# Turning quantised token and FFN rows with transposing DMAs in place of TensorE transposes

## The chip, the cores and the metric

The kernel runs on one core of a Trainium2 chip. The metric is the time of one execution on the device in microseconds (us); of a kernel that was run several times it is the median.

## The reference

`x` and `ctx` are [16, 256, 512] in float32. One cross-attention layer with 8 heads is followed by one FFN whose activations and weights are quantised. The heads split the rows of a batch element: head h takes rows 32h to 32h+31 of the queries, the keys and the values, and the attention is over the 512 columns.

```
def xattn(q, k, v):                     # q = layernorm(x), k = v = ctx
    qh, kh, vh = (a.reshape(16 * 8, 32, 512) for a in (q, k, v))
    sm = softmax(einsum('bdm,bdn->bmn', qh, kh) / sqrt(32), axis=-1)
    return einsum('bmn,bcn->bcm', sm, vh).reshape(16, 256, 512)

def act_quant(x):                       # per row: round(x * 127 / max|x|), scaled back
    scale = 127.0 / clip(max(abs(x), axis=-1, keepdims=True), 1e-5)
    return clip(round(x * scale), -128, 127) / scale

def bitlinear(x, w):                    # weights become -1, 0 or 1 times one scale
    return einsum('bsd,fd->bsf', act_quant(x), weight_quant(w))

x = x + xattn(layernorm(x), ctx, ctx)
x = x + bitlinear(silu(bitlinear(layernorm(x), W1)), W2)      # W1 [2048, 512], W2 [512, 2048]
```

## The kernel before, in words

The 4096 token rows are cut into 32 tiles of 128 rows (4 heads of 32 rows). A tile passes through these stages, and several tiles are in flight at once:

- Preparation: the tile of x and of ctx is loaded (`load`), x is normalised (`stats_x`, `aggregate`, `moments`, `rstd`, `xn`), ctx is scaled (`key_squares`, `key_norm`, `key_scale`, `key_rsqrt`), and both are split into two f16 parts (`qh`, `ql`, `kh`, `kl`), which small DMAs stack on partitions (`stack_qh` and the others).
- Maxima: 16 matmuls of 512 columns (`maxima`, tile mxp), each read by VectorE (`max_read`). The maxima of the rows are turned by one TensorE transpose (`ct`) and written back as two rows (`crow`) that the scores subtract.
- Scores: 16 matmuls into `st`, 16 exponentials on ScalarE, 8 pair sums on GpSimd (`sums`), the products with the values (`values`, tile pv) and the denominators (`denominators`, tile dn), then division (`invert`, `attend`), the residual sum on GpSimd (`residual`), and the second norm (`norm2`, `rstd2`, `xn2`).
- FFN: the row maximum (`absmax2`), a factor (`scale2`, `scale2_b`), `quantise` on GpSimd, the turn of the [128, 512] rows (`xqt`), a conversion to f16 on ScalarE (`xqt_evac`), four groups of four matmuls against W1 (`first`), `tanh` on ScalarE and `gate` on VectorE for each of the four parts, the maximum over all four (`hidden_max`, `hidden_scale` to `hidden_scale_d`), the quantisation of 2048 values a row, two parts of 512 on GpSimd (`hidden_quantise`) and two on ScalarE (`quantise_act`), the turn of [128, 2048] in two halves (`ht`, `ht_evac`), four groups of four matmuls against W2 (`second`), `rescale`, `finish`, `store`.

Each engine has its own instruction stream, written out by one loop: a tile has 16 units, one score matmul (TensorE) or exponential (ScalarE) in each, and the table `PLAN` says in which unit, counted from the first score of the tile, an engine carries out a step. A step at 28 lies in the second tile period after its own tile's first score. Within a unit the lists in `ORDER` decide. An engine takes its steps strictly in this order, and semaphores hold each until its inputs are there, so an engine's unit is a place in its queue and not a time. All DMAs are issued by the queue of the sync engine (SP), also in the order of the plan.

Before the change, quantising is the addition of a large constant (`MAGIC`), after which the low 16 bits of each float32 are an f16 number offset by 1536. TensorE turns these 128x128 blocks with an identity matrix into the PSUM bank `bank_a`: 4 blocks for the tokens, 8 for each half of the FFN rows. ScalarE then reads the bank, takes the offset off and writes f16 into `xqt` or `hqt`. The bank is shared with `key_norm`, `ct` and two of the four `first` groups, and the function `bank_free` puts a wait ahead of each use.

Of the kernel before, what the change touches and what calls it, by code (L numbers as in the profile page):

```python
# [6 lines left out]
B, S, D = 16, 256, 512  # L7
HEADS = 8
DH = S // HEADS
F = 2048  # L10
# [29 lines left out]
    key_squares=[-48],  # L40
    key_norm=[-41],
    stats_x=[-40],
    aggregate=[-39],
    rstd=[-41],
    xn=[-39],
    key_scale=[-41],
    kh=[-38],
    qh=[-31],
    kl=[-37],
    ql=[-35],  # L50
    maxima=[-22, -22, -21, -20, -20, -18, -17, -16, -15, -12, -11, -10, -10, -9, -8, -8],
    ct=[-6],
    ct_evac=[-6],
    ct_low=[-6],
    values=[13, 17, 19, 19],
    sums=[-2, 2, 4, 4, 6, 6, 6, 6],
    denominators=[17, 17],
    invert=[19],
    attend=[20],
    residual=[11],  # L60
    norm2=[21],
    norm2b=[23],
    rstd2=[17],
    xn2=[17],
    absmax2=[25],
    scale2=[25],
    quantise=[20],
    xqt=[27],
    xqt_evac=[26],
    first=[28, 28, 31, 32],  # L70
    tanh=[28, 28, 31, 32],
    gate=[29, 30, 32, 33],
    hidden_max=[30, 31, 34, 35],
    hidden_scale=[35],
    hidden_quantise=[26, 26],
    ht=[37, 39],
    ht_evac=[37, 39],
    second=[39, 40, 41, 42],
    finish=[39],
    max_read=[-22, -21, -21, -20, -20, -18, -18, -17, -13, -11, -11, -11, -10, -8, -7, -7],  # L80
    key_scale_b=[-3],
    moments=[-37],
    moments2=[24],
    scale2_b=[26],
# [3 lines left out]
    hidden_scale_c=[36],  # L88
    hidden_scale_d=[36],
    rescale=[42],  # L90
    quantise_act=[35, 37],
    key_rsqrt=[-46],
    load=[-56],
    load_v=[11],
    stack_qh=[-30],
    stack_kh=[-30],
    stack_ql=[-28],
    stack_kl=[-31],
    xr=[10],
    crow=[-2],  # L100
    store=[46],
# [5 lines left out]
    load=[-46, -43, -40, -35, -23, -20, -19, -19],  # L107
    rows=[-36, -35, -12, -9],
    abs=[-32, -25, -24, -24, -14, -9, -9, -7],
    sum=[-29, -7],  # L110
    quantise=[-24, -23, -22, -21, -7, -6, -5, 4],
    convert=[-23, -21, -16, -15, -4, -3, -1, 6],
# [4 lines left out]
ORDER = {'pool': ['xn', 'residual', 'rstd', 'hidden_quantise', 'key_rsqrt', 'rstd2', 'ql', 'quantise', 'sums',  # L117
          'xn2', 'finish'],
 'act': ['ht_evac', 'tanh', 'quantise_act', 'ct_evac', 'qh', 'kh', 'rescale', 'xqt_evac', 'key_squares'],
 'dve': ['hidden_scale_c', 'invert_b', 'scale2_b', 'gate', 'hidden_scale_d', 'key_scale_b', 'hidden_max',  # L120
          'max_read', 'kl', 'norm2', 'moments2', 'invert_c', 'key_scale', 'hidden_scale', 'absmax2',
          'moments', 'hidden_scale_b', 'norm2b', 'invert', 'stats_x', 'ct_low', 'attend', 'scale2',
          'aggregate'],
 'pe': ['key_norm', 'maxima', 'values', 'ct', 'xqt', 'first', 'denominators', 'second', 'ht'],
 'sp': ['xr', 'stack_kh', 'crow', 'stack_ql', 'store', 'stack_qh', 'load', 'stack_kl', 'load_v']}
# [41 lines left out]
def build(nc, x, ctx_in, values_t, w1t_in, w2t_in, out):  # L167
    f32 = mybir.dt.float32
    f16 = mybir.dt.float16
    ALU = mybir.AluOpType  # L170
# [10 lines left out]
    with stack:  # L181
# [32 lines left out]
        xqt = sb("xqt", [P, NC, P], f16)  # L214
# [79 lines left out]
        xqm_done = sem("xqm_done")  # L294
# [22 lines left out]
        xqt_done = sem("xqt_done")  # L317
# [6 lines left out]
        ht_done = sem("ht_done")  # L324
# [18 lines left out]
        def _(sp):  # L343
# [63 lines left out]
            def run(slot):  # L407
                steps = {"load": load, "load_v": load_values, "stack_qh": stack_qh, "stack_kh": stack_kh, "stack_ql": stack_ql,
                         "stack_kl": stack_kl, "xr": residual_rows, "crow": maxima_rows, "store": store}
# [14 lines left out]
            for b in range(-3, TILES + 3):  # L424
                run(Slot(b))
# [13 lines left out]
        BANK_A = uses(("key_norm", 0, key_clamped, 1, 1), ("ht", 0, ht_evac, 2, 1), ("ht", 1, ht_evac, 2, 2),  # L439
                      ("ct", 0, ct_low, 1, 1), ("xqt", 0, xqt_evac, 1, 1),  # L440
# [16 lines left out]
        def _(pool):  # L457
# [68 lines left out]
            def quantise(slot, off):  # L526
                r = slot.ring(off)
                wait(pool, token_scale, slot, 1, off, 1)
                pool.tensor_scalar(xqm[:, r % 2, :], xn2[:, :], sm2[:, r, SQ:SQ + 1], MAGIC, ALU.mult, ALU.add).then_inc(xqm_done, 1)

            def hidden_quantise(slot, off, n):

                if n == 0:
                    wait(pool, hidden_factor, slot, 1, off, 1)
                part = hu[:, 2 * n * D:(2 * n + 1) * D]
                pool.tensor_scalar(part, part, sm3[:, slot.ring(off), QS:QS + 1], MAGIC,  # L536
                                   ALU.mult, ALU.add).then_inc(hq_done, 1)
# [17 lines left out]
            for b in range(-3, TILES + 2):  # L555
                run(Slot(b))

        @block.scalar
        def _(act):
# [32 lines left out]
            def hidden_evac(slot, off, g):  # L592


                wait(act, ht_done, slot, 2, off, g + 1)
# [68 lines left out]
            for b in range(-3, TILES + 2):  # L664
                run(Slot(b))
# [332 lines left out]
```

## Time and profile before

| | |
|---|---|
| median of 3 runs | 803.3 us (802.32 to 803.55) |
| the profiled execution, its own time | 802.65 us |
| its span in the trace | 800.9 us |
| TensorE matmuls, busy | 724.1 us, 90% |
| VectorE, busy | 721.5 us, 90% |
| ScalarE, busy | 634.3 us, 79% |
| GpSimd, busy | 606.1 us, 76% |
| DMA queue of SP | 75.79 MB, 33.3% of the 16 engines |

PE is the matmul side of TensorE, PEld its weight load, DVE VectorE, ACT ScalarE, POOL GpSimd, SPq the queue of the sync engine. Busy shares are over the whole span, in which the first 60 us hold the weights' preparation and the last 36 us the drain of the pipeline. A matmul's record lasts longer than the distance to the next one, since matmuls are pipelined.

### The profile page before, as it was taken

How to read it: one execution, taken by the hardware profiler on the slowest of the kernel's cores; microseconds unless marked ns; L12 is line 12 of the kernel's file. 1: busy time of each engine (PE TensorE's matmuls, PEld its weight loads, DVE VectorE, ACT ScalarE, POOL GpSimd, SP SyncE). 2: the span in 40 equal slices, each digit the busy share in tenths (PEclk: the TensorE clock that was granted, in tenths of full speed). 3: DMA queues.
4: the chain of work that ended last, by engine and by line, in shares of the span. 5: the costliest groups of instructions: out<-in, count | busy, mean ns of one | idle time of the engine just before them, and what ended most of it. 6: DMA issues, size and time to landing. Idle time of an engine off the chain costs nothing.

```text
span 800.9 us, 13866 instructions
## 1 busy us (share of the span) xinstructions
PE 724.1 (90%) x4324; PEld 276.8 (35%) x4324; DVE 721.5 (90%) x1596; ACT 634.3 (79%) x1017; POOL 606.1 (76%) x619
## 2 busy tenths in 40 slices
PE   0349999999999999999999999999999999999984
PEld 0012233333333333333333333333333333333332
DVE  1898899999999999999999999999999999998552
ACT  4567688888888888888888888888888888877853
POOL 2215778888898888888889888888888988887861
PEclk9999899999999999999999999999999999999998
DMA  8553223233233333323323333333332333331100
GB/s 294 191 133 98 91 75 101 75 85 103 88 83 106 106 107 106 100 74 87 103 88 82 107 107 106 106 92 80 88 103 88 83 106 106 81 80 41 41 19 21
DMA packets 53960, 76.66 MB, mean 96 GB/s; under 512 B 7808, under 2 KB 32384, under 8 KB 52864
## 3 DMA queue, kind: packets, MB, share of 16 engines
q1 hardware_dynamic: 53888, 75.79, 33.3%
q8 instruction: 35, 0.57, 0.3%
q14 instruction: 37, 0.30, 0.1%
HBM read 41.94 MB, written 8.39 MB: 63 GB/s over the span
## 4 chain that ended last, share of the span: by engine, by line
PE 75%; DVE 8%; ACT 8%; issue 3%; DMA 3%; POOL 1%; SPq 1%; POOLq 0%; ACTq 0%; DVEq 0%
PE pv L893 15%; PE bank_b L924 13%; PE st L873 12%; PE mxp L883 11%; PE bank_b L953 7%; PE bank_a L953 7%; PE dn L902 7%; DVE mx L708 4%; ACT probs L569 4%; ACT late L596 3%; DMA late<-w 2%; PE bank_a L912 2%; PE bank_a L930 1%; DVE late L827 1%; DVE late L829 1%
## 5 line engine op out<-in xcount | busy, mean ns | idle before, releaser
L569 ACT ACTIVATE probs<-st,sm 128x512 f32<-128x512 f32 x512 | 333.7, 685 | 51.3 <-PE st L873 51.1
L502 POOL TENSOR_TENSOR sums<-probs 128x512 f32<-128x512 f32 x256 | 322.3, 1275 | 44.6 <-ACT probs L569 44.5
L708 DVE TENSOR_REDUCE mx<-mxp 128x1 f32<-128x512 f32 x512 | 335.1, 679 | 11.4 <-PE mxp L883 9.2
L883 PE MATMUL mxp<-ks,qs 96*128 96x512 f16 x512 | 195.5, 402 | 32.7 <-DVE mx L708 25.7
L873 PE MATMUL st<-qs,ks 98*128 98x512 f16 x512 | 195.0, 393 | 1.4 <-ACT probs L569 1.4
L924 PE MATMUL bank_b<-w2t,late 128*128 128x512 f16 x512 | 132.6, 382 | 3.0 <-ACT late L596 3.0
L893 PE MATMUL pv<-probs,vt 128*32 128x512 f32 x1024 | 130.6, 605 | 0.0
L883 PEld LDWEIGHTS mxp<-ks,qs 96*128 96x128 f16 x512 | 52.9, 104 | 117.3 <-DVE mx L708 87.1
L536 POOL TENSOR_SCALAR late<-late,sm 128x512 f32<-128x512 f32 x64 | 43.7, 696 | 60.4 <-DVE sm L808 60.4
L873 PEld LDWEIGHTS st<-qs,ks 98*128 98x128 f16 x512 | 47.8, 99 | 115.4 <-issue 55.3
L782 DVE TENSOR_REDUCE hmx<-late 128x1 f32<-128x512 f32 x128 | 83.4, 673 | 0.0
L596 ACT ACTIVATE late<-bank_a 128x1024 f16<-128x1024 f16 x64 | 65.6, 1025 | 13.7 <-PE bank_a L912 13.7
L924 PEld LDWEIGHTS bank_b<-w2t,late 128*128 128x128 f16 x512 | 49.4, 97 | 57.0 <-ACT late L596 4.9
L953 PE MATMUL bank_b<-w1t,xqt 128*128 128x512 f16 x256 | 66.3, 381 | 2.5 <-ACT xqt L612 1.8
L953 PE MATMUL bank_a<-w1t,xqt 128*128 128x512 f16 x256 | 65.7, 379 | 0.0
L902 PE MATMUL dn<-sums,ones 128*32 128x512 f32 x512 | 60.8, 592 | 0.0
L777 DVE SCALAR_TENSOR_TENSOR late<-late,bank_b 128x512 f32<-128x512 f32 x64 | 43.1, 674 | 14.9 <-ACT late L621 14.9
L590 ACT CAST qh<-xn 128x512 f16<-128x512 f32 x32 | 19.8, 618 | 41.7 <-POOL xn L485 41.7
L621 ACT ACTIVATE late<-bank_b,sm 128x512 f32<-128x512 f32 x64 | 44.0, 687 | 10.0 <-PE bank_b L953 8.3
L621 ACT ACTIVATE late<-bank_a,sm 128x512 f32<-128x512 f32 x64 | 44.0, 688 | 10.0 <-PE bank_a L953 7.2
L602 ACT ACTIVATE late<-late,sm 128x512 f32<-128x512 f32 x64 | 46.3, 723 | 6.2 <-DVE sm L808 6.2
L512 POOL TENSOR_TENSOR late<-att,xr 128x512 f32<-128x512 f32 x32 | 40.6, 1268 | 10.5 <-DVE att L733 10.5
(77 smaller groups left out, 913.4 us busy)
## 6 DMA issues: line engine op xcount, KB each, us to landing
cs<-ctx SPq DMA_DIRECT2D x32, 256.0 KB, 3.0
xs<-x SPq DMA_DIRECT2D x32, 256.0 KB, 3.6
late<-w SPq DMA_DIRECT2D x8, 1024.0 KB, 6.9
ks<-kh SPq DMA_DIRECT2D x64, 128.0 KB, 3.3
qs<-qh SPq DMA_DIRECT2D x64, 128.0 KB, 3.6
xr<-x SPq DMA_DIRECT2D x32, 256.0 KB, 4.1
vt<-values_t SPq DMA_DIRECT2D x32, 256.0 KB, 3.9
out<-late SPq DMA_DIRECT2D x32, 256.0 KB, 2.0
```

Source lines behind the costliest of these rows:

```text
L502: pool.tensor_tensor(sums[:, pair, h, :], probs[:, 2 * pair, h, :], probs[:, 2 * pair + 1, h, :], ALU.add).then_inc(sum_done, 1)
L569: act.activation(probs[:, c, h, :], st[u % 2][:, :], ACT.Exp, scale=sm1[:, r, ESC:ESC + 1]).then_inc(exp_done, 1)
L596: act.activation(hqt[:, FG // 2 * g:FG // 2 * (g + 1), :], bank_a[:, :].bitcast(f16).rearrange("p (c t) -> p c t", t=P), ACT.Copy, bias=-O ...
L621: act.activation(th[:, fc % 2, :], bank[:, :], ACT.Tanh, scale=sm2[:, slot.ring(off), HZ:HZ + 1]).then_inc(tanh_done, 1)
L708: dve.reduce_max(mx[:, slot.ring(off), NC * h + c:NC * h + c + 1], mxp[m % 2][:, :], axis=AX.X).then_inc(max_done, 1)
L782: dve.tensor_reduce(out=hmx[:, slot.ring(off), fc:fc + 1], in_=hu[:, fc * D:(fc + 1) * D], axis=AX.X, op=ALU.max, apply_absolute_value=Tru ...
L873: pe.matmul(st[u % 2][:, :], ks[0:3 * DH + 2, r, h, c * P:(c + 1) * P], qs[0:3 * DH + 2, r, h, :], start=True, stop=True).then_inc(st_done, 1)
L883: pe.matmul(mxp[m % 2][:, :], qs[0:3 * DH, r, h, c * P:(c + 1) * P], ks[0:3 * DH, r, h, :], start=True, stop=True).then_inc(mx_done, 1)
L893: last = pe.matmul(pv[DH * h:DH * (h + 1), :], vt[:, k, c, DH * h:DH * (h + 1)], probs[:, c, h, :], start=(c == 0), stop=(c == NC - 1), sk ...
L902: last = pe.matmul(dn[DH * h:DH * (h + 1), :], ones[:, 0:DH], sums[:, pair, h, :], start=(pair == 0), stop=(pair == 1), skip_group_check=True)
L924: last = pe.matmul(bank_b[:, :], hqt[:, f, :], w2t[:, f, :], start=(f == 0), stop=(f == FG - 1))
L953: last = pe.matmul(bank[:, :], xqt[:, j, :], w1t[:, j, fc * D:(fc + 1) * D], start=(j == 0), stop=(j == NC - 1))
```

## The change

The quantised rows are written as 16-bit integers (the conversion rounds), and DMAs on SP turn them from SBUF to SBUF. ScalarE reads the turned integers from SBUF and writes f16, for the tokens in place and for the FFN rows in place too. The 20 TensorE transposes of a tile and their use of `bank_a` are gone. One token DMA turns [128, 512], two hidden DMAs turn [128, 1024] each. New waits guard the buffers, and `PLAN`, `WEIGHTS` and `ORDER` are laid out anew.

```diff
+        xq = sb("xq", [P, 2, D], i16)
+        xqi = sb("xqi", [P, NC, P], i16)
+        xqt = xqi[:, :, :].rearrange("p c t -> p (c t)").bitcast(f16).rearrange("p (c t) -> p c t", t=P)
-        xqm = late[:, 8 * D:10 * D].rearrange("p (r d) -> p r d", d=D)
+        hq = late[:, 8 * D:10 * D].bitcast(i16)
+        hqi = late[:, 14 * D:16 * D].bitcast(i16).rearrange("p (g t) -> p g t", t=P)
...
+            def tokens_transpose(slot, off):
+                wait(sp, xq_done, slot, 1, off, 1)
+                wait(sp, f1_done, slot, FC, off - 1, FC)
+                sp.dma_start_transpose(out=xqi[:, :, :], in_=xq[:, slot.ring(off) % 2, :]).then_inc(xqt_landed, 16)
+            def hidden_transpose(slot, off, g):
+                wait(sp, hq_done, slot, 2, off, g + 1)
+                wait(sp, hqa_done, slot, 2, off, g + 1)
+                wait(sp, f2_done, slot, FC, off - 1, FC)
+                sp.dma_start_transpose(out=hqi[:, FG // 2 * g:FG // 2 * (g + 1), :],
+                                       in_=hq[:, F // 2 * g:F // 2 * (g + 1)]).then_inc(ht_landed[g], 16)
...
-                pool.tensor_scalar(xqm[:, r % 2, :], xn2[:, :], sm2[:, r, SQ:SQ + 1], MAGIC, ALU.mult, ALU.add).then_inc(xqm_done, 1)
+                wait(pool, xqt_landed, slot, 16, off - 2, 16)
+                pool.tensor_scalar(xq[:, r % 2, :], xn2[:, :], sm2[:, r, SQ:SQ + 1], 1.0, ALU.mult, ALU.mult).then_inc(xq_done, 1)
...
+                wait(pool, ht_landed[n], slot, 16, off - 1, 16)
+                pool.tensor_scalar(hq[:, part], hu[:, part], sm3[:, slot.ring(off), QS:QS + 1], 1.0,
+                                   ALU.mult, ALU.mult).then_inc(hq_done, 1)
...
-                act.activation(hqt[:, FG // 2 * g:FG // 2 * (g + 1), :], bank_a[:, :].bitcast(f16).rearrange("p (c t) -> p c t", t=P),
-                               ACT.Copy, bias=-OFFSET).then_inc(ht_evac, 1)
+                wait(act, ht_landed[g], slot, 16, off, 16)
+                act.copy(hqt[:, part, :], hqi[:, part, :]).then_inc(ht_evac, 1)
...
+                wait(act, ht_landed[n], slot, 16, off - 1, 16)
+                act.activation(hq[:, part], hu[:, part], ACT.Copy, scale=sm3[:, slot.ring(off), QS:QS + 1]).then_inc(hqa_done, 1)
...
+                wait(act, xqt_landed, slot, 16, off, 16)
+                act.copy(xqt, xqi[:, :, :]).then_inc(xqt_evac, 1)
...
-                    wait(dve, ht_done, slot, 2, off - 1, 2)
+                    wait(dve, hq_done, slot, 2, off - 1, 2)
+                    wait(dve, hqa_done, slot, 2, off - 1, 2)
```

The places in the plan of the steps that the prediction speaks of (before, then after):

```diff
-    values=[13, 17, 19, 19],          attend=[20],  residual=[11], quantise=[20],
+    values=[11, 17, 17, 17],          attend=[21],  residual=[18], quantise=[21],
-    xqt=[27],      xqt_evac=[26],     first=[28, 28, 31, 32],      gate=[29, 30, 32, 33],
+    xqt=[26],      xqt_evac=[26],     first=[28, 29, 31, 31],      gate=[30, 32, 33, 33],
-    hidden_quantise=[26, 26],         quantise_act=[35, 37],       hidden_scale_d=[36],
+    hidden_quantise=[31, 32],         quantise_act=[33, 34],       hidden_scale_d=[36],
-    ht=[37, 39],   ht_evac=[37, 39],  second=[39, 40, 41, 42],     store=[46],
+    ht=[35, 38],   ht_evac=[39, 40],  second=[40, 40, 41, 42],     store=[55],
-    load=[-56],    load_v=[11],       xr=[10],      crow=[-2],
+    load=[-54],    load_v=[9],        xr=[9],       crow=[-5],
```

In the order of SP's queue, the units of a period now hold: 0 `stack_qh`, `stack_ql`; 3 `ht` of the first half; 6 `ht` of the second; 7 `store`; 9 `xr`, `load_v`; 10 `load`, `xqt`; 11 `crow`; 12 `stack_kh`; 14 `stack_kl`.

## Rows read from the trace of the kernel before

**Rows 1.** The profile's page: busy time of the engines.

```profile
PE 724.1 (90%) x4324; PEld 276.8 (35%) x4324; DVE 721.5 (90%) x1596; ACT 634.3 (79%) x1017; POOL 606.1 (76%) x619
```

**Rows 2.** Busy time of each engine in stretches of time.

```profile
core 0: us, PE busy (x) PEld busy (x) DVE busy (x) ACT busy (x) POOL busy (x), PEclk, DMA share, GB/s
400.11:422.35 22.24, 21.82 (x137) 8.52 (x135) 21.75 (x50) 18.76 (x32) 18.69 (x20) 1.00 0.34 95
...
700.00:764.40 64.40, 61.74 (x388) 23.07 (x388) 48.52 (x112) 52.41 (x83) 50.31 (x50) 1.00 0.18 50
764.40:800.90 36.50, 22.75 (x134) 9.25 (x133) 14.69 (x37) 14.01 (x19) 13.51 (x14) 0.91 0.06 22
```

**Rows 3.** The chain that ended last, 400.11 to 422.35 us (start, length).

```profile
402.74 0.45 PE bank_a L912 x8
```

**Rows 4.** Waits of VectorE, 120 to 700 us (total, times, longest).

```profile
DVE mx L708 <- PE mxp L883: 5.8, 26, 0.2
```

**Rows 5.** Groups of instructions by line, whole span.

```profile
L912 PE MATMUL bank_a<-idh,late 128*128 128x128 f16 x512 | 39.9, 222 | 4.8 <-POOL late L536 4.8
L941 PE MATMUL bank_a<-idh,late 128*128 128x128 f16 x128 | 12.6, 221 | 0.6 <-POOL late L529 0.4 <-DVE crow L713 0.2
L596 ACT ACTIVATE late<-bank_a 128x1024 f16<-128x1024 f16 x64 | 65.6, 1025 | 13.7 <-PE bank_a L912 13.7
L612 ACT ACTIVATE xqt<-bank_a 128x512 f16<-128x512 f16 x32 | 19.1, 597 | 1.3 <-PE bank_a L941 1.2
L590 ACT CAST qh<-xn 128x512 f16<-128x512 f32 x32 | 19.8, 618 | 41.7 <-POOL xn L485 41.7
L529 POOL TENSOR_SCALAR late<-xn,sm 128x512 f32<-128x512 f32 x32 | 22.2, 695 | 1.2 <-DVE sm L767 1.2
L494 POOL TENSOR_TENSOR ql<-xn,qh 128x512 f16<-128x512 f32 x32 | 37.5, 1171 | 9.3 <-ACT qh L590 9.3
```

**Rows 6.** Timeline of one period: from the attention's division to the second FFN product.

```profile
398.58 0.69 DVE L733 TENSOR_TENSOR att<-pv,rden 128x512 f32<-128x512 f32 x1
...
406.38 0.69 POOL L529 TENSOR_SCALAR late<-xn,sm 128x512 f32<-128x512 f32 x1
...
408.86 1.03 PE L953 MATMUL bank_b<-w1t,xqt 128*128 128x512 f16 x4
...
401.71 1.03 PE L924 MATMUL bank_b<-w2t,late 128*128 128x512 f16 x4
...
419.81 0.13 DVE L808 TENSOR_SCALAR sm<-sm 128x1 f32<-128x1 f32 x1
```

**Rows 7.** DMA issues by line, KB each, median us from issue to landing.

```profile
xs<-x SPq DMA_DIRECT2D x32, 256.0 KB, 3.6
ks<-kl SPq DMA_DIRECT2D x32, 128.0 KB, 3.0
qs<-crow SPq DMA_DIRECT2D x64, 4.0 KB, 1.7
```

**Rows 8.** Landing times of the xr loads, the longest of the bulk in steady work.

```profile
DMA to landing us min/median/max: 2.7/4.1/4.6
```

**Rows 9.** Timeline of the last tile's drain.

```profile
777.31 0.69 POOL L529 TENSOR_SCALAR late<-xn,sm 128x512 f32<-128x512 f32 x1 [1.20 <-DVE sm L767]
...
779.15 1.04 PE L953 MATMUL bank_b<-w1t,xqt 128*128 128x512 f16 x4 [0.69 <-ACT xqt L612]
...
787.28 1.37 POOL L536 TENSOR_SCALAR late<-late,sm 128x512 f32<-128x512 f32 x2 [7.59 <-DVE sm L808]
...
790.18 1.89 PE L924 MATMUL bank_b<-w2t,late 128*128 128x512 f16 x4 [1.12 <-ACT late L596]
...
791.86 1.06 PE L912 MATMUL bank_a<-idh,late 128*128 128x128 f16 x8
...
792.72 3.55 PE L924 MATMUL bank_b<-w2t,late 128*128 128x512 f16 x12
```

More of the change, by code:

```diff
@@ L87 @@
     hidden_scale_b=[35],
-    hidden_scale_c=[36],
+    hidden_scale_c=[35],
     hidden_scale_d=[36],
     rescale=[42],
[L91 to L101, printed above, removed]
+    quantise_act=[33, 34],
+    key_rsqrt=[-42],
+    load=[-54],
+    load_v=[9],
+    stack_qh=[-32],
+    stack_kh=[-36],
+    stack_ql=[-32],
+    stack_kl=[-34],
@@ L102 @@
+    xr=[9],
+    crow=[-5],
+    store=[55],
 )
 WEIGHTS = dict(
[L107 to L112, printed above, removed]
-)
[L117 to L125, printed above, removed]
+    load=[-47, -43, -38, -37, -19, -18, -15, -9],
@@ new lines @@
+    rows=[-48, -31, -10, -9],
+    abs=[-39, -31, -31, -29, -15, -11, -10, -7],
+    sum=[-26, -4],
+    quantise=[-24, -21, -18, -13, -3, -2, 0, 3],
+    convert=[-21, -21, -14, -13, -7, -6, 2, 11],
+)
+ORDER = {'pool': ['rstd', 'hidden_quantise', 'ql', 'sums', 'residual', 'rstd2', 'finish', 'xn', 'key_rsqrt', 'xn2',
+          'quantise'],
+ 'act': ['qh', 'ct_evac', 'rescale', 'quantise_act', 'key_squares', 'ht_evac', 'xqt_evac', 'kh', 'tanh'],
+ 'dve': ['hidden_max', 'scale2_b', 'aggregate', 'max_read', 'stats_x', 'kl', 'invert_b', 'gate', 'ct_low',
+          'norm2', 'key_scale', 'absmax2', 'moments', 'scale2', 'hidden_scale', 'hidden_scale_d', 'invert',
+          'attend', 'norm2b', 'hidden_scale_b', 'moments2', 'key_scale_b', 'hidden_scale_c', 'invert_c'],
+ 'pe': ['first', 'maxima', 'denominators', 'key_norm', 'second', 'ct', 'values'],
+ 'sp': ['load', 'stack_qh', 'stack_ql', 'xqt', 'xr', 'ht', 'stack_kh', 'store', 'load_v', 'crow',
+          'stack_kl']}
@@ L423, in _ @@
                 fetch(Slot(t), 0)
-            for b in range(-3, TILES + 3):
+            for b in range(-3, TILES + 4):
                 run(Slot(b))
@@ L904, in denominators @@
                 last.then_inc(dn_done, 1)
-            def hidden_transpose(slot, off, g):
-                wait(pe, hq_done, slot, 2, off, g + 1)
-                wait(pe, hqa_done, slot, 2, off, g + 1)
-                bank_free(pe, BANK_A, slot, off, place("ht", g))
-                for j in range(FG // 2):
-                    f = FG // 2 * g + j
-                    last = pe.transpose(bank_a[:, :].bitcast(f16)[:, j * P:(j + 1) * P],
-                                        low_half(hu[:, f * P:(f + 1) * P]), idh[:, :])
-                last.then_inc(ht_done, 1)
             def second(slot, off, g):
@@ L935, in maxima_transpose @@
                 pe.transpose(bank_a[:, 0:P], mx[:, slot.ring(off), :], idf[:, :]).then_inc(ct_done, 1)
-            def tokens_transpose(slot, off):
-                wait(pe, xqm_done, slot, 1, off, 1)
-                bank_free(pe, BANK_A, slot, off, place("xqt", 0))
-                for j in range(NC):
-                    last = pe.transpose(bank_a[:, 0:D // 2].bitcast(f16)[:, j * P:(j + 1) * P],
-                                        low_half(xqm[:, slot.ring(off) % 2, j * P:(j + 1) * P]), idh[:, :])
-                last.then_inc(xqt_done, 1)
             def first(slot, off, fc):
```

121 lines of the change are left out of this document (57 added, 64 removed).

## The prediction

> **What bounds the kernel now.** I read the page first: TensorE and VectorE are both busy for 90% of the span, ScalarE and GpSimd clearly less [rows 1]. That is an average over ramp, steady work and drain, so the windows come next. One steady tile period is 22.24 us. In it PE is busy for 21.82 us and VectorE for 21.75 us [rows 2]: two engines stand almost wall to wall, with 0.42 and 0.49 us left, while ScalarE has 3.5 us and GpSimd 3.55 us of air. The clock is at full speed there (1.00, the 2.4 GHz level), so no gain is to be had from it in steady work.
>
> The chain of waits tells which of the two sets the pace. It runs on TensorE for most of the period, and the eight transposes of half the FFN rows occupy 0.45 us of it, 0.056 us each [rows 3]. That is much less than the 0.222 us that a record of one lasts [rows 5], since matmuls are pipelined: the 640 records sum to 52.5 us, but on the chain they are worth 640 x 0.056 = 36 us at the most. VectorE's own waits show the other side: over 26 periods it waited for TensorE only 26 times, for 5.8 us, all at the maxima [rows 4]. The rest of its 0.49 us are short gaps between its own dependent instructions.
>
> **The change part by part.**
>
> *Removed from TensorE.* Two halves of 0.45 us and the tokens' four blocks, 4 x 0.056 = 0.22 us: 1.12 us a period. TensorE could then run a period in 22.24 - 1.12 = 21.12 us. VectorE gets no instruction less: a gate waits for the quantisers instead of the transposes, that is all. So VectorE is next, at 21.75 us plus its own gaps. What can be had in steady work is its wait for TensorE, 5.8 / 26 = 0.22 us a period, over 26 periods -5.8 us. Bounds: 0 (the wait turns into another one of the same length), and all of the 0.49 us, 26 x 0.49 = -12.7 us. I take -5.8, the wait that names TensorE.
>
> *Last scores, 700 to 764 us.* No maxima are left, VectorE is busy for 48.5 of 64.4 us, PE for 61.7 [rows 2]. Two to three tiles' transposes lie on the path; at 1.12 us each, two tiles are -2.2 us. ScalarE and GpSimd at 52 and 50 us are not far off and their order is changed, so I take half, -1.1, between 0 and -2.2.
>
> *Conversions.* ScalarE reads SBUF in place of PSUM. A cast of 512 columns from SBUF takes 618 ns against 597 from PSUM [rows 5]: 0.02 us more for the tokens, at twice the width 0.04 for each half, 0.1 us a period, which its 3.5 us of air take; without them it would be 26 x 0.1 = 2.6 us. GpSimd writes 16-bit integers instead of f32; no row shows this form. The f16 output of the nearest operation with conversion is not slower (1171 ns for ql, with two inputs), so I keep 695 ns; the upper bound is 1171, +0.48 us for each of three, 1.4 us a period out of 3.55 us of air.
>
> *Added to SP's queue.* Three issues a period. The existing ones go out in 0.35 to 0.65 us, about twelve of them are 7 us of 22, so three more fit, if an issue is like the others. `xqt` and `ht` wait for their quantisers. Behind `ht` stand `store`, `xr`, `load_v` and `load`, which are read a tile or more later; behind `xqt` stands `crow`, five units ahead of the scores that need it (about 7 us against 1.7 us of landing [rows 7]). I cost these at nothing; the cover is that lead.
>
> *Added to the latency.* This is the part that decides. Before, the tokens' quantised rows are ready at 407.07, and the first product starts at 408.86 [rows 6]. From the division (399.27) to that product are 9.6 us, of which 7.8 go by to the end of the quantiser. In the new plan the last values' products stand two units earlier (17 for 19) with `first` still at 28; a unit is 22.24 / 16 = 1.39 us, so some 2.5 us are won and 12.1 us are there. Less 7.8, and less 0.6 for the conversion, the DMA may take about 3.7 us. For the FFN rows: the factor is ready at 419.94 and the second product starts at 401.71 + 22.24 = 423.95 [rows 6], 4.0 us later; with the last `first` one unit earlier and `second` one later there are 6.7 us, less 0.7 for quantising and 1.1 for conversion: about 4.9 us for the landing.
>
> No row shows a transposing DMA. Bounds from the plain ones: 1.7 us (the 4 KB rows) to 4.6 us (the longest bulk load) [rows 7, 8]. The tokens' 128 KB are nearest to the stack of kl, 128 KB in SBUF, 3.0 us; the halves' 256 KB to the load of xs, 3.6 us [rows 7]. I take 3.0 and 3.5. Both fit their places, with 0.7 and 1.4 us to spare. ScalarE, which takes the conversion in order ahead of later exponentials, may wait for it; its air covers that up to the same limit.
>
> One rule of the Trainium skill speaks against this. "VectorE: DVE Perf Modes", section "The three transpose paths", gives 390 ns to a 128x128 block on TensorE and 1309 ns to one by DMA, and advises TensorE where PSUM will do. Our row of a TensorE transpose, 222 ns, is shorter still; if the blocks of a DMA came one after the other at that figure, the tokens' four would be an estimated 5.2 us and a half's eight 10.5 us. "Advanced Engine Details and Errata", section "X-Bar Transpose (TRN2)", says the opposite of the rate: as fast as regular DMAs, which would leave my 3.0 and 3.5 us. No row here decides between them.
>
> *The drain.* The last tile is one chain, in which the longer latency is not hidden. Tokens: from the quantiser's end at 778.00 to the product at 779.15 are 1.15 us [rows 9]; with 3.0 + 0.6 + 0.1 it is 3.7, +2.6 us. FFN rows: the first part is ready at 787.97, the product starts at 790.18, 2.2 us; with 3.5 + 1.0 + 0.2 it is 4.7, +2.5 us. The transposes amid the second product go, 791.86 to 792.72: -0.85 us. Together +4.3 us. With 1.7 and 4.6 us for both DMAs it would be +1.2 and +7.0.
>
> *Sum.* -5.8 - 1.1 + 4.3 = -2.6 us, on the profiled execution's 802.65 us (span 800.9 and 1.75 around it): 800.05. That execution lay 0.65 below the median of 803.3, so 800.7 is what I forecast for the median. Its own range: -12.7 - 2.2 + 1.2 gives 789.6, and 0 + 0 + 7.0 gives 810.3; the middle of it, 795 to 806, holds most.
>
> **The rivals.**
>
> *A: the tokens' DMA lands after its place (slower).* Place: ScalarE's `xqt_evac`, then `first`. What speaks for it: SP issues `xr`, `load_v` and two loads of 256 KB just ahead of `xqt`; bulk loads in such a row land up to 4.6 us after issue [rows 8], above the 3.7 us. And a 16-bit turn moves small pieces. Against: the loads may have drained when the quantiser is ready. It decides from 3.7 us on: each microsecond above it holds `first`, `tanh`, `gate` and with it VectorE back once a period, 29 periods or so. At 4.6 us: 0.9 x 29 = +26 us in place of -5.8, with the drain's +6 about 829 us; at 5.2 us about 848. It begins gently, at about 806.
>
> *B: the turn is slow in itself or occupies SP for long (slower by much).* If the halves need 8 us, 3.1 above their 4.9, each period grows by that: 29 x 3.1 = +90 us, some 900 us. The share of the DMA engines, 0.34 [rows 2], gives no ground for it, but no row excludes it. This is where the first rule of the skill above would lead.
>
> *C: the full gain.* VectorE closes all its gaps thanks to the new order, and the drain costs little: 790 to 794 us. Against: most of its gaps follow from its own dependences, which are unchanged.
>
> *D: integer output is slow on GpSimd.* With +1.4 us a period GpSimd is at 20.1 of 22 us, which alone fits, but 0.48 us come off each of the two places above; it then acts as rival A does and shares its chance.
>
> **How the numbers follow.** A difference of 0.2%, 1.6 us, is about what a measurement of this kernel can tell from none. My forecast holds 0.48 (of it 0.28 below 801.7 us, 0.12 between 801.7 and 804.9, 0.08 above). A with D has 0.37, all slower, mostly between 806 and 848. B has 0.10, C 0.05. Faster 0.33, same 0.12, slower 0.55: the single likeliest case is a small gain, but more of the chance lies on the side of a loss, since the gain is capped by VectorE and the loss by nothing. The range reaches from 793 to 845: it leaves out C's half, B, and the end of A.
>
> **What would show it.** Right: a period between 21.8 and 22.1 us, VectorE at 99% of it, PE at 95% or less, no wait for PE at the maxima, landings of about 3 and 3.5 us, the drain after the last score some 4 us longer. Wrong: ScalarE waiting for `xqt` or the FFN rows' DMA in each period, VectorE waiting for tanh at the first gate (A); landings above 5 us or transposing issues of several us on SP (B); records of the quantisers on GpSimd well above 0.7 us (D). The step most likely to fail is the landing time, which I had to take from DMAs that turn nothing.

## The result, and the profile after

The changed kernel takes 862.7 us (median of 4, 859.9 to 866.1) against 803.4 us before: 1.073 times as long (95% interval 1.071 to 1.076). The forecast was 800.7 us with a range of 793 to 845. The landing times of the new DMAs came out close to what was forecast; the period did not.

The page of the changed kernel answers to [rows 1]; its second part shows the clock.

```profile
PE 757.2 (88%) x3684; PEld 244.8 (28%) x3684; DVE 709.9 (82%) x1596; ACT 640.4 (74%) x1017; POOL 608.7 (71%) x619
...
PEclk9999799999999999999999999999999999999887
```

PE carries out 640 matmuls less and is busy 33 us longer. VectorE fell from 90% to 82% of the span: it isn't the bound that the prediction took it for. In a steady period it is busy for 21.1 to 21.3 us, against 21.75 before [rows 2], with the same instructions; the section on one_block says why. Two periods of the changed kernel, the third tile's and a later one, by the view of stretches (columns as in [rows 2]):

```profile
136.15:158.85 22.70, 21.52 (x117) 7.26 (x115) 21.10 (x50) 18.90 (x32) 18.80 (x19) 1.00 0.50 127
231.25:255.15 23.90, 22.84 (x116) 7.61 (x115) 21.20 (x50) 18.91 (x32) 18.81 (x19) 0.93 0.47 117
```

They hold the same instructions. The second is 1.2 us longer, and what differs is the granted clock, 1.00 against 0.93. The starts of the residual sums, one a tile, lie 22.8, 22.7, 22.7 us apart at the beginning, then 24.2, 24.2, 24.0, 24.0 and 23.9 to the end of steady work (22.24 before). Seven of the sixteenths of one such period show where the clock goes:

```profile
398.76:400.25 1.49, 0.98 (x5) 0.23 (x4) 1.49 (x3) 1.49 (x4) 1.26 (x1) 1.00 1.28 154
400.25:401.75 1.50, 1.46 (x5) 0.28 (x5) 1.43 (x6) 1.50 (x3) 0.14 (x1) 1.00 0.78 151
401.75:403.24 1.49, 1.12 (x4) 0.23 (x3) 1.42 (x3) 1.49 (x3) 1.38 (x3) 0.67 0.98 259
403.24:404.74 1.50, 1.50 (x5) 0.50 (x4) 1.47 (x7) 1.12 (x3) 1.20 (x2) 0.50 0.95 354
404.74:406.23 1.49, 1.49 (x6) 0.57 (x5) 1.49 (x3) 0.81 (x1) 1.49 (x2) 0.69 0.79 205
406.23:407.72 1.49, 1.49 (x9) 0.66 (x8) 0.65 (x2) 0.67 (x1) 1.49 (x3) 1.00 0.76 190
407.72:409.22 1.50, 1.50 (x9) 0.77 (x8) 0.78 (x2) 1.05 (x4) 1.50 (x2) 1.00 0.05 10
```

The granted clock is 1.00 (2.4 GHz), falls to 0.50 (1.2 GHz) and returns within 4 us. Ahead of the fall, PE has only four or five matmuls in 1.5 us. In the low stretch stand the first eight matmuls of the second FFN product; the timeline (start, length) has them as

```profile
404.03 2.70 PE L934 MATMUL bank_b<-w2t,late 128*128 128x512 f16 x8
```

and the chain of waits as

```profile
404.24 2.50 PE bank_b L934 x8
```

2.50 us for eight, where four take 0.86 us at full clock. That is 0.8 of the 1.2 us; the scores and maxima in the low stretch take longer as well. Right behind, VectorE, which had been the busy one, runs dry: in the timeline

```profile
405.69 0.68 DVE L691 BATCH_NORM_STATS2 bn<-xs 128x6 f32<-128x512 f32 x1
407.21 0.69 DVE L727 TENSOR_REDUCE mx<-mxp 128x1 f32<-128x512 f32 x1 [0.84 <-PE mxp L903]
408.62 0.69 DVE L727 TENSOR_REDUCE mx<-mxp 128x1 f32<-128x512 f32 x1 [0.72 <-PE mxp L903]
```

From 240 to 700 us it waited for the maxima's matmuls 46.7 us in all, 2.4 us a period, against 5.8 us in 26 periods in [rows 4]. Not all of that is the clock: in fill_8 (below), whose clock stays at 1.00, 28.5 us of it remain, 1.4 us a period. First the changed kernel, then fill_8:

```profile
DVE mx L727 <- PE mxp L903: 46.7, 80, 1.0
...
DVE mx L728 <- PE mxp L904: 28.5, 60, 0.7
```

The new operations, by groups of instructions:

```profile
L556 POOL TENSOR_SCALAR late<-late,sm 128x512 int16<-128x512 f32 x64 | 43.6, 695 | 12.5 <-DVE sm L828 12.1
L615 ACT CAST late<-late 128x1024 f16<-128x1024 int16 x64 | 66.2, 1035 | 6.2 <-DMA late<-late 6.2
L549 POOL TENSOR_SCALAR xq<-xn,sm 128x512 int16<-128x512 f32 x32 | 22.2, 693 | 9.1 <-DVE sm L786 8.3
```

and the new DMAs, in the page's part on DMA issues (median us from issue to landing at the end):

```profile
late<-late SPq DMA_TRANSPOSE x64, 3.2
xqi<-xq SPq DMA_TRANSPOSE x32, 2.9
```

ScalarE waited for a transposing DMA four times in the whole execution, 6.2 us together. Integer output costs GpSimd nothing (695 and 693 ns against 695 in [rows 5]).

**Where the 60.8 us of the span are.** By the residual sums: start of the first one +3.1 us; three first periods +1.2; 26 steady periods +44.1, that is some 12 from the nearly 0.5 us by which even a period at full clock is longer, and 32 from the clock; the last two periods +5.6; from the last residual sum to the end +6.8 (35.5 against 28.8).

### The profile page after: what moved, and what is told of

The parts are those of the page before. It is cut to its first block, busy times and chain, and to the rows that moved or that the text cites. A ratio compares the mean times of both kernels' runs of the same rounds, so it can differ in the third digit from the quotient of the medians.

```text
span 861.7 us, 12835 instructions
## 1 busy us (share of the span) xinstructions
PE 757.2 (88%) x3684; PEld 244.8 (28%) x3684; DVE 709.9 (82%) x1596; ACT 640.4 (74%) x1017; POOL 608.7 (71%) x619
## 2 busy tenths in 40 slices
DMA packets 138950, 97.58 MB, mean 113 GB/s; under 512 B 92800, under 2 KB 117376, under 8 KB 137856
## 4 chain that ended last, share of the span: by engine, by line
DVE 50%; PE 39%; issue 6%; DMA 2%; POOL 2%; ACT 1%; SPq 0%; POOLq 0%; ACTq 0%
DVE mx L727 17%; PE bank_b L934 15%; PE mxp L903 9%; DVE late L797 8%; DVE hmx L802 8%; PE st L893 6%; PE pv L913 5%; PE bank_b L955 3%; DVE att L752 2%; DVE bn L757 2%; DVE dspread L738 2%; DVE rden L746 2%; DMA late<-w 2%; DVE late L849 1%; DVE late L847 1%
## 5 line engine op out<-in xcount | busy, mean ns | idle before, releaser
L520 POOL TENSOR_TENSOR sums<-probs 128x512 f32<-128x512 f32 x256 | 322.4, 1272 | 29.7 <-ACT probs L589 28.9
L903 PE MATMUL mxp<-ks,qs 96*128 96x512 f16 x512 | 206.4, 431 | 40.1 <-DVE mx L727 39.3
L934 PE MATMUL bank_b<-w2t,late 128*128 128x512 f16 x512 | 156.0, 448 | 14.2 <-ACT late L615 14.2
L934 PEld LDWEIGHTS bank_b<-w2t,late 128*128 128x128 f16 x512 | 57.5, 113 | 99.0 <-issue 44.6
L622 ACT ACTIVATE late<-late,sm 128x512 int16<-128x512 f32 x64 | 45.6, 716 | 44.2 <-DVE sm L828 44.2
L615 ACT CAST late<-late 128x1024 f16<-128x1024 int16 x64 | 66.2, 1035 | 6.2 <-DMA late<-late 6.2
L490 POOL TENSOR_TENSOR sm<-sm,half 128x1 f32<-128x1 f32 x32 | 19.5, 609 | 70.2 <-DVE sm L704 70.2
L955 PE MATMUL bank_b<-w1t,xqi 128*128 128x512 f16 x256 | 65.8, 378 | 2.0 <-ACT xqi L632 1.3
L955 PE MATMUL bank_a<-w1t,xqi 128*128 128x512 f16 x256 | 66.0, 380 | 0.0
L535 POOL TENSOR_TENSOR sm<-sm,half 128x1 f32<-128x1 f32 x32 | 17.6, 549 | 50.1 <-DVE sm L770 50.1
L562 POOL TENSOR_TENSOR late<-late 128x512 f32<-128x512 f32 x32 | 41.3, 1292 | 15.9 <-ACT late L649 15.9
L556 POOL TENSOR_SCALAR late<-late,sm 128x512 int16<-128x512 f32 x64 | 43.6, 695 | 12.5 <-DVE sm L828 12.1
```

Source lines behind the costliest of these rows:

```text
L520: pool.tensor_tensor(sums[:, pair, h, :], probs[:, 2 * pair, h, :], probs[:, 2 * pair + 1, h, :], ALU.add).then_inc(sum_done, 1)
L615: act.copy(hqt[:, part, :], hqi[:, part, :]).then_inc(ht_evac, 1)
L903: pe.matmul(mxp[m % 2][:, :], qs[0:3 * DH, r, h, c * P:(c + 1) * P], ks[0:3 * DH, r, h, :], start=True, stop=True).then_inc(mx_done, 1)
L934: last = pe.matmul(bank_b[:, :], hqt[:, f, :], w2t[:, f, :], start=(f == 0), stop=(f == FG - 1))
L955: last = pe.matmul(bank[:, :], xqt[:, j, :], w1t[:, j, fc * D:(fc + 1) * D], start=(j == 0), stop=(j == NC - 1))
```

## The experiments

Each kernel ran against the kernel before on the same chip. "Period" is the distance of the residual sums' starts in steady work (where it varies, its range and the mean of the 26 periods from the fourth on), "clock" the mean granted one there.

| run | us | ratio to before (95%) | period, us | clock |
|---|---|---|---|---|
| changed kernel | 862.7 | 1.073 (1.071 to 1.076) | 23.9 | 0.93 |
| small_copy | 855.8 | 1.064 (1.061 to 1.067) | 23.9 | 0.93 |
| plain_copy | 857.0 | 1.066 (1.063 to 1.069) | 22.7 and 23.9 | 1.00 and 0.93 |
| fill_8 | 828.5 | 1.031 (1.029 to 1.034) | 22.7 | 1.00 |
| fill_old | 838.6 | 1.044 (1.042 to 1.046) | 23.2 | 1.00 |
| fill_gap | 840.6 | 1.046 (1.042 to 1.049) | 23.1 | 1.00 |
| fill_late | 868.1 | 1.080 (1.076 to 1.083) | 23.8 | 1.00 |
| one_block | 790.5 | 0.983 (0.981 to 0.985) | 21.74 | 1.00 |
| tokens_only | 865.2 | 1.074 (1.070 to 1.078) | 22.9 to 25.2, mean 24.2 | 0.98 |
| hidden_only | 1012.8 | 1.260 (1.258 to 1.262) | 28.8 to 30.2 | 0.86 to 0.89 |
| pe_after_plan | 1008.3 | 1.255 (1.253 to 1.257) | 28.3 and 29.7 in turn | 0.91 |
| values_spread | 972.6 | 1.210 (1.208 to 1.213) | 27.4, some up to 28.9 | 0.89 to 0.92 |
| replan_fill | 877.3 | 1.091 (1.088 to 1.094) | 23.9 to 25.9, mean 24.3 | 0.99 |
| replan_nofill | 890.1 | 1.106 (1.103 to 1.109) | 23.5 to 26.9, mean 25.1 | 0.94 |
| replan2_fill | 933.1 | 1.158 (1.152 to 1.164) | 24.5 to 28.4, mean 26.1 | 0.94 |
| replan3_fill | 825.5 | 1.026 (1.024 to 1.028) | 22.1 to 23.7, mean 22.5 | 1.00 |
| replan3_nofill | 839.5 | 1.043 (1.039 to 1.047) | 22.1 to 24.2, mean 22.9 | 0.98 |
| replan4_fill | 835.7 | 1.037 (1.033 to 1.041) | 22.8 to 24.4, mean 23.1 | 1.00 |

### Are the DMAs themselves the cost? plain_copy and small_copy

```diff
-                sp.dma_start_transpose(out=xqi[:, :, :], in_=xq[:, slot.ring(off) % 2, :]).then_inc(xqt_landed, 16)
+                part = slice(0, D if slot.b + off == 0 else 8)          # small_copy; plain_copy: all of D
+                sp.dma_start(xqi[:, :, :].rearrange("p c t -> p (c t)")[:, part], xq[:, slot.ring(off) % 2, part]).then_inc(xqt_landed, 16)
```

and the same for the two DMAs of the FFN rows. Both leave the turn out, so the FFN works on other values; queues and waits stay.

> The changed kernel with plain DMAs of the same bytes in place of the transposing ones (the rows aren't turned, so the FFN's values are wrong; sizes, queues and waits stay). If transposing as such costs time (issue of 1.25 us in place of 0.6, small packets, DMA share 0.48): faster by 5 us or more. If plan, clock and place in the period are the cause: within 3 us of the changed kernel, 860 to 866.

> The changed kernel with plain DMAs of 16 bytes a partition in place of the transposing ones (from the second tile on; the FFN's values are wrong), which should land in about 2 us in place of 2.9 and 3.2 and load the DMA engines hardly at all. If the landing time sets the period: 2 x 1 us a period come back, 800 to 830. Plan and clock theory: the period stays at 23.5 to 23.9 us, and only the drain gets some 2 to 3 us shorter: 850 to 860.

The DMA issues of small_copy:

```profile
late<-late SPq DMA_DIRECT2D x62, 2.0 KB, 1.8
...
xqi<-xq SPq DMA_DIRECT2D x31, 2.0 KB, 1.7
```

and two of its periods, by the view of stretches:

```profile
400.00:423.90 23.90, 22.99 (x116) 7.52 (x115) 21.32 (x50) 18.98 (x32) 18.81 (x19) 0.93 0.30 89
423.90:447.80 23.90, 22.98 (x116) 7.52 (x115) 21.33 (x50) 18.97 (x32) 18.82 (x19) 0.93 0.32 90
```

The landings are 1.2 and 1.4 us shorter, the DMA share falls from 0.48 to some 0.31, and the period is 23.90 us as in the changed kernel, to the hundredth. With this plan, landing time, packets, load and the time of issue of the transposing DMAs have no part in the steady loss; they are worth the 7 us by which the whole gets shorter, nearly all of it after the last residual sum (30.0 us against 35.5). That sinks the prediction's rivals A and B, and the first of the rules it weighed: "VectorE: DVE Perf Modes" of the Trainium skill, section "The three transpose paths", would have made four blocks 5.2 us; the measured DMA of four blocks lands after 2.9 us, issue included.

plain_copy is 5.7 us faster than the changed kernel, which by its expectation spoke for a cost of the turn itself. By the residual sums it comes from the start (2.4 us), from three more periods that stay short (3.5) and from the end (3.3), not from a shorter steady period. It shows something else. Its periods switch between two lengths in one execution, with the same instructions (the view of stretches again):

```profile
204.70:227.40 22.70, 21.51 (x117) 7.28 (x115) 21.09 (x51) 18.93 (x32) 18.80 (x19) 1.00 0.43 123
...
296.90:320.90 24.00, 22.92 (x117) 7.61 (x115) 21.25 (x51) 19.00 (x32) 18.79 (x19) 0.93 0.38 116
```

### Is it the clock? fill_gap, fill_old, fill_8, fill_late

Transposes of the identity are added, into the half of the bank `dn` that nothing reads then. Only their number and place differ: 7 in each of the units 3 to 7 (fill_gap); 8, 8 and 4 in units 5, 7 and 11, where the removed ones had been (fill_old); 4 and 4 in units 4 and 6 (fill_8); 10 and 10 in units 9 and 11 (fill_late).

```diff
+            def fill(slot, off, n):
+                wait(pe, dn_spread, slot, 1, off - 1, 1)
+                for j in range((4, 4)[n]):
+                    pe.transpose(dn[:, D // 2:].bitcast(f16)[:, (j % NC) * P:(j % NC + 1) * P], idh[:, :], idh[:, :])
```

> The changed kernel with 35 extra 128-column TensorE transposes of the identity a period (7 in each of the units 3 to 7, into the unused half of bank dn; the output is unaffected). Clock theory (the thin stretch of TensorE in units 2 to 7 makes the granted clock fall, and the second FFN product that follows runs at half speed, 1.65 us a period): the clock stays at 1.00 in steady work, the period falls from 23.9 to about 22.3 us, the time to 810 to 825. Order theory (too much TensorE work is crowded into units 8 to 15 and VectorE starves there at any clock): period 23.5 us or more, 855 or more. DMA theory (transposing DMAs delay their readers or the stacks): unchanged, 860 to 866, or slower by the work added.

> The changed kernel with 20 extra transposes of the identity a period, as many as the change took away and at their old places (8 in unit 5, 8 in unit 7, 4 in unit 11), into the unused half of bank dn. If the removed transposes by themselves kept the clock up: as fill_gap, 810 to 825. If the thinness comes from the moved values' products rather than from the transposes: the clock still falls, 855 to 865. DMA theory: 860 to 870.

> The changed kernel with 8 transposes of the identity a period, 4 in unit 4 and 4 in unit 6. If 0.45 us of work in the thin stretch hold the clock: period 22.7 to 22.9 us (the changed kernel's own period where its clock was 1.00, tiles 2 and 3, is 22.7), 825 to 832 in all. If it takes more to hold it: still 0.93 and 23.9 us, 860 to 866.

> The changed kernel with 20 transposes of the identity a period, as many as in fill_old, but 10 in unit 9 and 10 in unit 11, where TensorE is dense. Place theory: the thin stretch stays thin, the clock falls as in the changed kernel, and the added 1.1 us lie on the path: 24.5 to 25.5 us a period, 880 to 915. Count theory (matmuls in a period hold the clock wherever they are): clock 1.00, 23.2 to 23.9 us, 838 to 862.

A period of fill_8:

```profile
400.00:422.70 22.70, 21.79 (x127) 7.75 (x126) 21.09 (x51) 18.89 (x32) 18.78 (x20) 1.00 0.53 122
```

With 0.45 us of useless work a period (eight transposes at the 0.056 us of [rows 3]), the clock stays at 1.00 and the kernel is 34 us faster than the changed one. Its period, 22.7 us, is that of the changed kernel's own first periods. So the clock's fall costs 1.2 us a period, about 31 us over the 26 steady ones, and this is shown by adding work alone. fill_gap and fill_old fell short of their expected 810 to 825 us: the clock held, but the period stayed above 23 us, of which 0.4 to 0.5 are due to the added work. One of my own expectations fell too: I had put the fall down to the thin stretch alone. In fill_late that stretch is as thin as ever and the clock still stayed at 1.00; only its 1.1 us of work lie on the path (22.7 + 1.1 = 23.8), which puts its time between the ranges of both theories:

```profile
400.00:424.00 24.00, 22.82 (x139) 8.37 (x135) 21.28 (x51) 19.27 (x33) 18.97 (x21) 1.00 0.47 118
```

What keeps the clock up is therefore not settled by these runs. Shown are that it falls in the thin stretch, that it does so in some periods and not in others with the same instructions (plain_copy: three to five matmuls in 1.5 us ahead of the second FFN product in both), and that in this plan added TensorE work in either place prevented it. It is no general cure: in replan2_fill, another plan, the clock fell to 0.50 in spite of 20 added transposes a period (0.94 in the mean).

### What is removing the transposes worth? one_block

The kernel before, with 3 of the 20 transposes of a tile left, so the FFN works on other values.

```diff
-                for j in range(FG // 2):
+                for j in range(1):
...
-                for j in range(NC):
+                for j in range(1):
```

> The kernel before with only one of the 8 or 4 transposes of each turn carried out; the conversions read that one block for all, so the FFN's inputs are wrong in value while every wait, read and write stays. It is what removing the transposes alone is worth, with no DMA and the plan unchanged (17 of 20 gone). By the prediction's step: TensorE has 0.95 us less a period and VectorE sets the pace, 22.0 us a period, 795 to 798 in all. If thinning TensorE by itself brings the clock down: a dip in each period, 805 or more. If VectorE's waits don't shrink: 803.

A period of one_block, by the view of stretches:

```profile
394.91:416.65 21.74, 20.94 (x120) 7.60 (x118) 20.99 (x50) 18.59 (x32) 19.13 (x19) 1.00 0.35 97
```

and its group of instructions for `kl`:

```profile
L702 DVE SCALAR_TENSOR_TENSOR kl<-cs,sm,kh 128x512 f16<-128x512 f32 x32 | 23.9, 748 | 0.7 <-ACT kh L583 0.7
```

It comes out faster than expected: 790.5 us, 0.983 of before. The period falls by 0.50 us, where I had 0.22. VectorE's waits for the maxima account for that 0.22; its busy time falls as well, from 21.75 to 20.99 us, although it has the same instructions. Nearly all of this is one instruction: `kl` took 1464 ns on average before and takes 748 ns here. So the 0.50 us is not the freed TensorE time alone: without the transposes `kl` also starts at another place beside GpSimd's work.

What that place does can be read in the timelines (start, length). In the kernel before, `kl` starts 1.0 us ahead of the end of a pair sum on GpSimd; in replan3_fill it starts 0.9 us ahead in one period and 0.2 us ahead in another:

```profile
407.04 2.49 POOL L502 TENSOR_TENSOR sums<-probs 128x512 f32<-128x512 f32 x2
408.50 1.58 DVE L702 SCALAR_TENSOR_TENSOR kl<-cs,sm,kh 128x512 f16<-128x512 f32 x1
...
376.42 1.27 POOL L550 TENSOR_TENSOR sums<-probs 128x512 f32<-128x512 f32 x1
376.75 1.49 DVE L751 SCALAR_TENSOR_TENSOR kl<-cs,sm,kh 128x512 f16<-128x512 f32 x1
...
217.87 1.29 POOL L550 TENSOR_TENSOR sums<-probs 128x512 f32<-128x512 f32 x1
218.93 0.79 DVE L751 SCALAR_TENSOR_TENSOR kl<-cs,sm,kh 128x512 f16<-128x512 f32 x1
```

Each time `kl` ends 0.55 us behind the sum. In nine traces there are 223 `kl` that start with 0.2 us or more of a two-input GpSimd operation on 128x512 left to run, and all of them end 0.54 to 0.56 us behind it, whatever their own length; with nothing beside it, one takes 0.74 us. It also goes the other way: in one_block at 403.65 us `kl` takes 0.74 us, and the sum that starts 0.13 us after it is recorded with 1.74 us in place of 1.27. No run moves `kl` alone, but the lengths leave little else. The changed plan is clear of this too (`kl` 765 ns, VectorE 0.65 us a period less than before), so VectorE had more room than the prediction gave it, and the period still grew.

The clock is 1.00: with the plan of before, taking the work away doesn't bring it down.

### Is it the plan? values_spread, pe_after_plan, hidden_only, tokens_only

```diff
-    values=[11, 17, 17, 17],
+    values=[11, 17, 19, 19],      # values_spread: the changed kernel, nothing else
```

pe_after_plan is the kernel before with the changed plan (`xqt` at 27, `ht` at 39 and 40 on TensorE). hidden_only and tokens_only keep the plan of before and turn one of the two by DMA.

> The changed kernel with two of the four groups of values' products moved from unit 17 to unit 19 (values = 11, 17, 19, 19; before the change 13, 17, 19, 19), which puts 16 real matmuls into the thin stretch. Clock theory: the stretch is fuller, the dip shorter or gone, 815 to 845, though the division comes some 2 us later and the tokens' DMA lands nearer to its reader. Order theory: some gain too, from less crowding is none here (unit 17 isn't the crowded part): 860. If the later division holds up the FFN: above 866.

> The kernel before, TensorE transposes and PSUM reads as they were, with the changed kernel's plan and orders (the turns at units 27, 39 and 40 of TensorE, no transposing DMA). If the new plan is the cause, by its thin stretch: slow too, 845 to 875, with a clock dip. If the DMAs are the cause: 800 to 815.

> The plan of before, the tokens turned by TensorE, only the FFN rows (two DMAs a tile, landing 3.2 us) by DMA. In the old plan the second FFN product starts 4.0 us after the factor, of which 1.8 are quantising and conversion, so the DMA is about 1 us late: latency theory 22.24 + 1 us a period, 825 to 845, at full clock or with a dip on top (up to 1.6 us more, 870). If the lateness is absorbed: 800 to 808.

> The plan of before, the FFN rows turned by TensorE, only the tokens by DMA (landing 2.9 us). In the old plan quantised tokens are read by the first product 1.8 us after they are ready, 0.6 of it the conversion; the DMA is about 1.8 us late: latency theory 22.24 + 1.8 us a period, 850 to 870. If ScalarE's and GpSimd's air absorb part: 810 to 850; if all: 800 to 806.

All four are slow. pe_after_plan and hidden_only are far beyond every range given for them, and values_spread is 106 us above the "above 866" of its third case. They show how little such a plan forgives. In values_spread, VectorE's `attend` stands in its queue where the products used to be ready; it now waits for them 36.1 us in 300 to 600 us, eleven times:

```profile
DVE att L752 <- PE pv L913: 36.1, 11, 4.4
```

In hidden_only it is the landing that counts, and the conversion, in order on ScalarE, holds up the exponentials behind it:

```profile
ACT late L606 <- DMA late<-late: 76.9, 21, 6.0
```

The period grows by 7 us against the 1 us that I had worked out, with a clock of 0.86 to 0.89. Each DMA lands 3.1 us after its issue, but the two stand in a row on SP, `ht` of the second half behind that of the first, and both conversions stand close behind. tokens_only costs what the latency theory said: 1.9 us a period in the mean, where it had 1.8. In pe_after_plan the turns and their conversions share one bank and follow each other: in 300 to 600 us ScalarE waits 59.2 us for the FFN rows' turns, and VectorE 82.1 us for the maxima; the shared bank as the cause is argued, not tried. It says that the changed plan doesn't suit the old way of turning, and nothing on the DMAs. The two ways each need a plan of their own, so the change can't be split into plan and DMA by exchanging the parts.

### New plans for the DMA version: replan_fill, replan_nofill, replan2_fill, replan3_fill, replan3_nofill, replan4_fill

The kernel stays the changed one; `PLAN` and `ORDER` are laid out anew from the durations in the traces. "fill" has 20 transposes of the identity in units 4, 5 or both (in replan4_fill 4 and 7). The core of the third plan:

```diff
-    first=[28, 29, 31, 31],      gate=[30, 32, 33, 33],      second=[40, 40, 41, 42],
+    first=[28, 29, 31, 32],      gate=[29, 30, 32, 32],      second=[38, 39, 40, 42],
-    values=[11, 17, 17, 17],     denominators=[15, 17],      ht_evac=[39, 40],
+    values=[11, 16, 17, 17],     denominators=[16, 16],      ht_evac=[36, 38],
```

> Transposing DMAs as in the changed kernel, with a new plan (the values' products at units 16, 17, 18, 18, first at 28, 29, 30, 31, second at 39, 39, 41, 42, and others), and 20 transposes of the identity in unit 4 to hold the clock. Order theory: VectorE no longer starves in units 9 to 12, period 22.0 to 22.3 us, 803 to 815 in all; the drain stays 7 us longer. If the DMAs cost something that no plan avoids: 830 or more.

> replan_fill without the 20 extra transposes. Clock theory: units 2 to 7 now hold some of the values' products, but are still thin; a dip in each period of up to 1 us would give 815 to 835; if the moved products suffice to hold the clock: as replan_fill, 800 to 813.

> A second, independent new plan for the transposing DMAs, with the extra transposes. Order theory: within 1% of replan_fill. If that one's gain were an accident of one plan: anywhere.

> Transposing DMAs with a third plan: first at units 28, 29, 31, 32, second at 38, 39, 40, 42, values at 11, 16, 17, 17, gates one unit earlier, 20 transposes of the identity in units 4 and 5. Order theory: period 22.1 to 22.4 us, the drain still 7 us longer, 808 to 818. If something of the DMA version holds any plan back: period 23 us or more, 835 or more.

> replan3_fill without the extra transposes. With second beginning in unit 6 and first ending in unit 0, only units 2 to 5 are thin: clock theory in its mild form, no or a short dip, 808 to 820; if any stretch with neither FFN products nor transposes brings the clock down for some us: 825 to 840.

> A fourth plan, found apart from the third, with the extra transposes. Order theory: period 22.2 to 22.5 us, 810 to 822. Otherwise 835 or more.

The first two plans missed by far (877.3 for 803 to 815, 933.1 for within 1% of that): they had been laid out with half the time of the values' and denominators' products, whose f32 matmuls each leave two records in the trace. With that put right, the third reaches, at its best,

```profile
345.00:367.10 22.10, 21.57 (x135) 8.54 (x135) 21.67 (x51) 18.78 (x32) 19.06 (x20) 1.00 0.48 126
```

a period of 22.1 us, below the 22.24 of before, with all three transposing DMAs in it. So nothing in the DMA version as such holds the period at 22.7 us or more; the order does. Which part of the order is argued, since the third plan moves many steps at once, and most likely is the place of the FFN's products in the queues. In the changed plan, eight matmuls of `second` stand in unit 8, eight more in units 9 and 10, then values and `first`, and VectorE gets its maxima one by one with nothing else to do, while in units 2 to 7 TensorE waits for VectorE. The third plan has `second` in units 6, 7, 8 and 10 and `first` up to unit 0.

In all, replan3_fill is still 2.6% slower than before, and above its expected 808 to 818 us. Of the 24.5 us of its span, 7.9 are the start, 7.8 the 26 periods, which take 22.5 us in the mean and up to 23.7 at clock 1.00, 2.4 the last two periods and 6.4 the end. In one of the long periods, 206.8 to 230.5 us, the landing shows:

```profile
ACT late L645 <- DMA late<-late: 2.1, 1, 2.1
```

A plan with `ht_evac` at 36 instead of 39 leaves less room for the landing of the FFN rows' DMAs, whose median is 3.4 us in this run; ScalarE waits for them 29 times in the whole execution, 24.3 us, where the changed kernel has four times and 6.2 us. So the DMA isn't free in this plan: the room for its landing has been given back for a shorter period. Without the extra transposes (replan3_nofill) it is 14 us slower, at a clock of 0.98. replan4_fill, 835.7 us, missed its 810 to 822 as well and lies where its expectation put a cost that no plan avoids; the short periods of replan3_fill speak against that, but neither plan settles it for the whole. No version with transposing DMAs was found that beats the kernel before.

## Why the prediction was wrong

- **The step that failed** is the first of the change's parts: "VectorE is next", and with it that a period is what the busier of two engines needs. It gave -5.8 us for 26 steady periods; measured are +44.1, some 12 from the new order at full clock and 32 from the clock, which the prediction had put at nothing. Taking the transposes away alone does gain (one_block: -0.50 us a period, -13.6 us in all, `kl` included), but the changed plan lost more than that. With TensorE and VectorE each at 21 to 22 us of a 22 us period, the order in which they hand work to each other sets the period, and I read the new order only for latencies, not for where each engine would be left without work. At full clock that costs 22.7 - 21.74 = 0.96 us a period against one_block, nearly 0.5 against before; VectorE's waits for the maxima's matmuls, which were to vanish from 0.22 us a period, are 1.4 us there (fill_8). Nor was 21.75 us VectorE's floor: it contained some 0.8 us in which `kl` stood behind GpSimd, and a period of the changed kernel needs 21.1.
- **The clock.** "No gain is to be had from it" was right and beside the point: a loss was to be had. PE stood at 98% [rows 2] and nothing in the trace of before showed a fall in steady work, but the stretches with waiting did show lower clocks (0.91 in the drain [rows 2]). I had a rival for each late DMA and none for this. It is the largest term, some 32 us, shown by fill_8. Why the clock falls here stays open.
- **DMA landings**: 2.9 and 3.2 us against my 3.0 and 3.5. Close, and the places in the plan were wide enough: from the tokens' quantiser to their conversion there are 4.9 us (405.25 to 410.11) where I had 3.7, and ScalarE waited for the new DMAs four times in all. Rivals A and B did not happen. Issues on SP take 1.2 to 1.9 us where I took 0.6; small_copy, which issues in 0.5, shows that the period doesn't depend on it.
- **Conversions, integer output**: 600 and 1035 ns on ScalarE, 693 and 695 ns on GpSimd; rival D fell, the term was as small as forecast.
- **The drain**: forecast +4.3 us, measured +6.8 from the last residual sum. For the tokens the last quantised row was ready at 832.0, the product started at 837.66, 5.6 us where I had 3.7; the landing of this one is the longest of all tokens' DMAs, 4.6 us, and ScalarE's conversion also stood behind `rescale`, which waited for the tile before it. The FFN rows' 4.4 us from the first part (846.5) to the product (850.86) are as forecast (4.7). The 0.85 us that the missing transposes were to give back in the last tile's second FFN product did not come: it takes 6.26 us against 6.1 before, at a granted clock of 0.57 against 0.66.
- **The last two periods**, forecast -1.1 us, measured +5.6: the granted clock there is 0.92 and 0.85, and 1.00 in the same stretch before [rows 2]. The clock is about half of it: in fill_gap and fill_old it is 1.00 in both periods, and they are still 3.1 and 3.3 us longer than before, the added work included.
- **The bounds**: the range's upper end, 845, came from A alone. The end where the reordering itself loses had no price in it. A slip in A's sum changes little: the 829 us follow if the 26 us come on top of the -5.8, and with "in place of" it would be some 834. That the size of the landings was met while the time was missed by 62 us shows how little the result hung on the step called most likely to fail.

## What to carry to other kernels

Where two engines fill a period almost wholly, work taken from one of them is worth something only if the order leaves neither waiting; read a new order for each engine's empty stretches, not only for the latencies that it has to hide. Work on TensorE may pay for itself through the clock: look at the granted clock in slices of the period before and after anything is moved off TensorE, and try the effect with a few useless transposes, which takes one run. Check the long two-input instructions of VectorE against GpSimd's timeline: here one of them stood 0.8 us a period behind a sum, and looked busy. A long latency in an in-order pipeline costs little by itself if the plan has room for it, but the room comes out of the order of everything else and out of the drain.

## What the runs showed of the hardware

- A transposing DMA from SBUF to SBUF of 128x512 in 16 bits lands 2.9 us after its issue (2.4 to 4.6), one of 128x1024 3.2 us (3.0 to 4.9). Plain ones of the same sizes took 2.1 and 2.6 us (plain_copy). Packets under 512 B rose from 7,808 to 92,800 and the DMA share from 0.34 to 0.48, with no effect on the period (small_copy).
- One instruction stream had two stable periods, 22.7 us at clock 1.00 and 23.9 us at 0.93, and switched between them in one execution (plain_copy).
- VectorE's `kl`, 128x512 with two full inputs, takes 0.74 us alone. Started while a two-input GpSimd operation of 128x512 is running, it ends 0.54 to 0.56 us after that one's end (223 of 223 in nine traces), so up to 1.6 us.
- Eight useless 128x128 transposes a period, 0.45 us, kept the granted clock at 1.00 where it had fallen to 0.50 for some 3 us of each period (fill_8 against the changed kernel); twenty did not in another plan (replan2_fill, 0.94).
